# A decoder block on Trainium2: x_proj's B computed by columns, the skip term added through a diagonal matrix, and more scan steps with a row-wise dt·u·B

## The reference: a Mamba pair, an attention, eight experts

```python
u, z = split(x @ in_w.T)                    # 512 channels each
u = silu(causal_dwconv(u, cw, cb))          # 4 taps
dt, Bm, C = split(u @ xp_w.T)               # 16, 64 and 64 columns
dt = softplus(dt @ dtw.T + dtb)             # 512 channels
A = -exp(A_log)                             # 512 x 64
def step(h, (u_t, dt_t, B_t, C_t)):
    h = h * exp(dt_t[:, None] * A) + (dt_t * u_t)[:, None] * B_t[None, :]
    return h, h @ C_t
y = scan(step) + u * D_skip
y = y * silu(z)
out = y @ out_w.T
```

## Time and profile before

| | before |
|---|---|
| median of 3 runs | 3466.93 us |
| profiled execution, its own time | 3468.26 us |
| its span | 3466.5 us |
| mean granted TensorE clock | 0.907 of full speed |
| busy share: VectorE, ScalarE, GpSimd, TensorE | 90%, 81%, 78%, 77% |
| busy VectorE, of which scans, products | 3132.8 us, 2313.6, 710.5 |
| first scan begins, last scan ends | 45.35 us, 3248.9 us |

### The profile page before, as it was taken

How to read it: one execution, slowest core, us unless ns; L and a number is a source line. 1 busy time by engine, 2 the same in 40 slices (tenths; PEclk the granted TensorE clock), 3 DMA queues, 4 the chain that set the end, 5 groups by cost and what they waited for, 6 DMA issues and landing times.

```text
span 3466.5 us, 50869 instructions
## 1 busy us (share of the span) xinstructions
PE 2655.7 (77%) x17556; PEld 2274.8 (66%) x17556; DVE 3132.8 (90%) x2269; ACT 2795.2 (81%) x6418; POOL 2707.2 (78%) x1335
## 2 busy tenths in 40 slices
PE   5767676787777788788787777878878778888876
PEld 3666565666656667677676666767767666777766
DVE  4999999999999999999999999999999999999610
ACT  6979899887989798887888868888797968887422
POOL 5889888887989788787878878787887978877501
PEclk7889998988899899899899988999999879899988
DMA  2242111111111133222242122413323123343486
GB/s 97 86 138 65 46 47 49 52 47 52 47 47 48 48 113 100 81 84 95 73 143 77 68 92 77 140 62 98 122 81 119 50 73 114 99 141 125 136 267 191
DMA packets 148758, 319.64 MB, mean 92 GB/s; under 512 B 25466, under 2 KB 41859, under 8 KB 147988
## 3 DMA queue, kind: packets, MB, share of 16 engines
q1 hardware_dynamic: 144546, 305.60, 26.8%
q0 software_dynamic: 3072, 8.39, 0.7%
q10 hardware_dynamic: 882, 2.38, 0.2%
HBM read 286.42 MB, written 29.88 MB: 91 GB/s over the span
## 4 chain that ended last, share of the span: by engine, by line
issue 32%; DVE 24%; POOL 20%; ACT 12%; PE 11%; DMA 1%; SPq 0%; POOLq 0%; DVEq 0%; ACTq 0%
POOL hC L919 17%; DVE h L1159 11%; DVE psX L1149 10%; ACT dA L1127 5%; ACT xs L1102 2%; PE psY L1422 2%; PE psX L1406 2%; PE psG L1374 2%; PE psX L1374 1%; POOL scratch L832 1%; PE psG L1450 1%; PE psX L1450 1%; DVE gT L1174 1%; POOL gT L842 0%; POOL dtu L855 0%
## 5 line engine op out<-in xcount | busy, mean ns | idle before, releaser
L919 POOL TENSOR_TENSOR hC<-h,cb 128x1024 f32<-128x1024 f32 x1024 | 2405.9, 2366 | 535.0 <-DVE h L1159 526.8
L1159 DVE TENSOR_TENSOR_SCAN h<-dA,psX 128x1024 f32<-128x1024 f32 (+1 forms) x1113 | 2313.6, 2107 | 70.9 <-PE psX L1406 41.9
L1127 ACT ACTIVATE dA<-dt,negA 128x255 f32<-128x255 f32 x4096 | 1717.5, 501 | 124.4 <-DVE h L1159 120.4
L1422 PE MATMUL psY<-ident,hC 128*128 128x128 f32 x8192 | 1186.4, 293 | 61.4 <-DVE gT L1174 41.4
L1422 PEld LDWEIGHTS psY<-ident,hC 128*128 128x128 f32 x8192 | 1041.3, 153 | 96.2 <-DVE gT L1174 44.9
L1406 PE MATMUL psX<-ident,xs 128*128 128x128 f32 x3488 | 537.5, 305 | 300.2 <-ACT xs L1102 150.8
L1149 DVE TENSOR_TENSOR psX<-dtu,psX 128x1024 f32<-128x1024 f32 x588 | 710.5, 1208 | 60.2 <-POOL dtu L855 37.1
L1406 PEld LDWEIGHTS psX<-ident,xs 128*128 128x128 f32 x3488 | 440.3, 156 | 399.7 <-ACT xs L1102 227.4
L1102 ACT ACTIVATE xs<-dtuT,bT 128x512 f32<-128x512 f32 x872 | 579.8, 717 | 9.9 <-PE psX L1406 9.3
L1397 PE MATMUL psX<-bparts,sel 96*128 96x256 bf16 x588 | 172.8, 294 | 238.5 <-DVE h L1159 230.3
L1397 PEld LDWEIGHTS psX<-bparts,sel 96*128 96x128 bf16 x588 | 59.7, 102 | 349.9 <-DVE h L1159 322.0
(11 more groups left out here) (217 smaller groups left out, 1880.1 us busy)
## 6 DMA issues: line engine op xcount, KB each, us to landing
cb<-c_dram SPq DMA_DIRECT2D x256, 512.0 KB
w_up<-in_w_exp SPq DMA_DIRECT2D x198, 256.0 KB
w_down<-in_w_exp SPq DMA_DIRECT2D x198, 256.0 KB
dA<-in_w_exp SPq DMA_DIRECT2D x42, 256.0 KB, 4.2
h<-in_w_exp SPq DMA_DIRECT2D x42, 256.0 KB, 4.4
x_slots<-got SPq DMA_DIRECT2D x16, 512.0 KB, 5.4
xg<-x_slots SPq DMA_DIRECT2D x60, 128.0 KB
y_slots<-yg SPq DMA_DIRECT2D x60, 128.0 KB
```

What stands on the lines that cost most here:

```text
L919: eng.tensor_tensor(hC[i % NHC][:, :, :], h[i % NH][:, :, :], cw.to_broadcast([P, KI, L]), ALU.mult).then_inc(times_c, 1)
L1127: made = eng.activation(dA[j % NA][:, c, 1:L], dt[n % 2][:, c, 1:L], ACT.Exp, scale=negA[:, JOBS[n][0], c, s:s + 1])
L1159: made = eng.tensor_tensor_scan(h[i % NH][:, part, :].rearrange("p c t -> p (c t)"), dA[i % NA][:, part, :].rearrange("p c t -> p (c t)"), ...
L1422: made = eng.matmul(psY[:, tc, c * P:(c + 1) * P], hC[i % NHC][:, c, tc * P:(tc + 1) * P], ident[:, :], start=s == 0 and c == 0, stop=Fals ...
```

## The change

Four edits. B is now computed with positions on the partitions (64 columns, two chunks of positions), and one copy by ScalarE makes `bT` of it; the three bf16 parts, their two GpSimd subtractions, five ScalarE copies, `b_turn` and `sel` are gone. In a plain step `spread_b` takes its row from `bT`: a transpose whose input is the column B_s repeated 128 times, once for each half of the positions. The skip term is added by real f32 products of u with a diagonal matrix of D (`diag`, made once at the start by ScalarE), in the middle of a job, and u is no longer scaled; `gate` waits for the last sum instead. The shares rise to 18 of 30 and 14 of 30: 511 turned steps (221 in the first six jobs, 290 after), and in the first six jobs 70 of them come right behind another turned step. w_x is loaded in three DMAs, which take from the unchanged array only the columns that are used.

```diff
-SHARE = [15] * 6 + [12] * (NJ - 6)
+SHARE = [18] * 6 + [14] * (NJ - 6)
...
-            task("b", n, 0, "PE", 2 * MM, ("silu", n, 0), opens="G"),
-            task("b+", n, 0, "PE", 2 * MM, ("b", n, 0)),
-            task("b", n, 1, "PE", 2 * MM, ("b+", n, 0)),
-            task("b+", n, 1, "PE", 2 * MM, ("b", n, 1)),
-            task("b_hi", n, 0, "ACT", 2 * EVICT, ("b+", n, 1), *((("b_rest", n - 1, 0),) if n else ()), frees=("b", n, 0)),
-            task("b_rest", n, 0, "POOL", 1200, ("b_hi", n, 0)),
-            task("b_mid", n, 0, "ACT", EVICT, ("b_rest", n, 0)),
-            task("b_rest2", n, 0, "POOL", 1200, ("b_mid", n, 0)),
-            task("b_lo", n, 0, "ACT", 2 * EVICT, ("b_rest2", n, 0))]
+            task("b", n, 0, "PE", 8 * TURN, ("silu", n, 0), opens="G"),
+            task("b+", n, 0, "PE", 8 * TURN, ("b", n, 0)),
+            task("bT_copy", n, 0, "ACT", 330, ("b+", n, 0), frees=("b", n, 0))]
...
-    out.append(task("skip", n, 0, "ACT", 4 * HALF_EVICT, ("dtu", n, 1), ("c_copy", n, 0), ("b_hi", n, 0)))
...
-                    at["PE"] = sum_end[j] = max(at["PE"], c_end[j]) + SUM * (2 if j % S == S - 1 else 1)
+                    at["PE"] = sum_end[j] = max(at["PE"], c_end[j]) + SUM * (3 if j % S == S // 2 else 1)
...
-            eng.dma_start(w_x[:, :, :, :], io["w_x"]).then_inc(mamba_in, 16)
+
+            for to, at, many in ((0, 0, HALF), (HALF, 3 * HALF, HALF), (S, 6 * HALF, S + R)):
+                eng.dma_start(w_x[:, :, :, to:to + many], io["w_x"][:, :, :, at:at + many]).then_inc(mamba_in, 16)
...
-                        k, at = turn["b_turn", n, 0]
+                        k, at = turn["b", n, 0]
                         on.wait_ge(full[k], at + 1)
+                        on.wait_ge(x_in, S * (n - 1))
                         eng.activation(bT[n % 2][:, :, :], bank[k][:, 0:KL * S].rearrange("p (a s) -> p a s", a=KL),
                                        ACT.Copy).then_inc(free[k], 1)
...
-                    elif name == "skip":
-                        on.wait_ge(dtu_done, 2 * (n + 1))
-                        for c in range(KI):
-                            made = eng.activation(u[n % 2][:, c, :], u[n % 2][:, c, :], ACT.Identity,
-                                                  scale=dskip[:, JOBS[n][0], c:c + 1])
-                        made.then_inc(skipped, 1)
...
+            on.wait_ge(set_up, SETUP + 1)
+            for l in range(LAYERS):
+                for c in range(KI):
+                    made = eng.activation(diag[:, l, c, :], ident[:, :], ACT.Copy, scale=dskip[:, l, c:c + 1])
+            made.then_inc(diag_made, 1)
...
-                on.wait_ge(b_lo_done, n + 1)
+                evicted(("b", n, 0))
                 on.wait_ge(scanned, i - 1)
-                eng.matmul(psX[i % 2][:, KI - 1, :], sel[:, s % HALF:s % HALF + 1].to_broadcast([3 * HALF, P]), bparts[n % 2][:, s // HALF, :],
-                           start=True, stop=True).then_inc(x_in, 1)
+                for tc in range(KL):
+                    made = eng.transpose(psX[i % 2][:, KI - 1, tc * P:(tc + 1) * P], bT[n % 2][:, tc, s:s + 1].to_broadcast([P, P]), ident[:, :])
+                made.then_inc(x_in, 1)
...
             def add_skip(n):
-                on.wait_ge(skipped, n + 1)
+                on.wait_ge(diag_made, 1)
+                on.wait_ge(silued, n + 1)
                 for tc in range(KL):
                     for c in range(KI):
-                        made = eng.matmul(psY[:, tc, c * P:(c + 1) * P], u[n % 2][:, c, tc * P:(tc + 1) * P], ident[:, :],
-                                          start=False, stop=True, is_transpose=True, skip_group_check=True)
-                    made.then_inc(y_done, 1)
+                        eng.matmul(psY[:, tc, c * P:(c + 1) * P], u[n % 2][:, c, tc * P:(tc + 1) * P], diag[:, JOBS[n][0], c, :],
+                                   start=False, stop=False, skip_group_check=True)
...
-                        made = product(dst[0:3 * HALF, part * L:(part + 1) * L],
-                                       [(w_x[:, l, c, part * 3 * HALF:(part + 1) * 3 * HALF], u[n % 2][:, c, :])
-                                        for c in (2 * i, 2 * i + 1)], not second, second)
-                        if part == i == 1:
+                        made = product(dst[:, i * S:(i + 1) * S], [(u[n % 2][:, c, i * P:(i + 1) * P], w_x[:, l, c, 0:S]) for c in range(KI)])
+                        if second:
                             made.then_inc(full[k], 1)
...
                 if j >= 0:
+                    if j % S == S // 2:
+                        add_skip(j // S)
                     sum_states(j)
-                    if j % S == S - 1:
-                        add_skip(j // S)
```

78 lines of the change are left out of this document (14 added, 64 removed).

## The result

The changed kernel takes **3389.56 us** (median of 4 runs, 3385.51 to 3395.4) beside 3467.88 us (median of 4, 3465.08 to 3469.7) for the kernel before: ratio 0.9774, 95% interval 0.9761 to 0.9788. The profiled execution took 3395.4 us, its span is 3393.7 us, and the mean granted clock rose from 0.907 to 0.928. It is the slowest of the four, 5.8 us above the median, so a few us in a stretch of one trace can be the execution and not the kernel.

A forecast was written before the change was run, and what follows sets the result against it. VectorE was taken to bound the loop (97.0% busy in the first six jobs, 96.6% after). From 3468.3 us, loop -70, head -4 and tail 0 give 3394, less 1.3 to the median: 3393 us, range 3362 to 3436.

The forecast's parts named there:

- The mechanism: In the loop VectorE sets the pace; 75 products fewer remove 90.6 us of its work, 70 us of it gained.
- rival on the slower side: Two, early jobs: TensorE's clock stays low (3554 us, chance 0.03); turned pairs stall 2.13 us each (3542 us, 0.04).
- The early jobs: First six jobs: VectorE's work falls to 1078.3 us, idle share 4.5%, giving 1129 us, a gain of 26 us.
- The pair: Two turned steps in a row, 70 times early: nearly free, 0.1 us each, bounds 0 and 2.13 us.
- take over as the bound: Rival in the early jobs: ScalarE, 1031 against VectorE's 1078 us, bounds them; 26 us lost, 3419 us, chance 0.15.
- The late jobs: Last ten jobs: VectorE's work falls to 1931.3 us, idle share 3.7%, giving 2005 us, a gain of 44 us.
- beside scans, so this shortens nothing by itself: Loop: removing B's chain on ScalarE (76.4 us) and GpSimd (about 37 us) gains nothing directly, only room for scalings.
- The skip, valued at nothing: Skip term moved from a job's last step into step 32: 0 us, bounds -18 and +35 us.
- The tail: After the last scan: three expert tiles more, partly hidden; 0 us against 217, between -8 and +24 us.
- full dovetailing: Tail: expert tiles fill TensorE's gap after the last scan, 209 us against 217, -8 us.
- The head: Uncovered chain before the first scan: shorter B product, one small copy, one subtraction gone; -4 us, bounds -1 and -6.
- three terms valued at nothing: B's chain in the loop, the skip's move into step 32 and the tail, each taken as 0 us.

The follow-up runs named there:

- b_alone: Kernel before with only B by columns and the transposed spread; old shares, old skip term and scaled u kept: 3444.37 us, 0.9923 of the kernel before.
- skip_end_old_plan: Changed kernel with only the issue of the skip products moved to a job's last step, planner's allowance left in place: 3379.47 us, 0.9735 of the kernel before.
- late_share: Changed kernel with shares 15 of 30 in the first six jobs and 14 in the others, only late shares raised: 3409.55 us, 0.9835 of the kernel before.

## Why the prediction came out as it did

The forecast was 3393 us (range 3362 to 3436), the result 3389.56 us.

**The mechanism was right.** VectorE set the pace, and what left it came off the loop. Products 513 and 619.2 us (forecast 513, about 620), scans 2306.7 (2314), ScalarE 2805.8 (2820), the scan's psX waits 56.7 us (50 to 80), the skip 31.8 us (35). The loop ended near 3156 us, 19 us before the 3175 of the forecast, and for that the tail was 20 us longer. Neither rival on the slower side came: the clock rose, and the pairs cost 0.37 us, below the point of about 1 us where they would decide.

**The early jobs, right, with the reason shifted.** -22.7 us for -26. The idle share is 59.8/1132.3 = 5.3%, I took 4.5%. The pair was the mis-sized term, 0.1 us against 0.37. The working found a pair free even with turns of 1.97 us, because it gave TensorE nothing else to do. But 12 of the 21 us at second steps came at step 4, where the turns are queued behind the sum that waits for the gate and then run at the lower clock (1.91 us at 241.69 in job 1). The 2.2 to 2.6 us at step 28 of four jobs are the wait behind the SiLU that the earlier trace rows had shown once; here the second step of the pair often waits 1.1 us more. ScalarE did not take over as the bound: it is busy 90.1% of the stretch. The 96% of the prediction was a share of VectorE's work, and by that measure it is 95% (1019.9/1072.2).

**The late jobs, mis-sized: -69.7 us for -44.** I let the idle share rise from 3.4 to 3.7%; it fell to 2.4%. The path through the runs: B alone -24.0 us (2048.5 to 2024.5), skip edit +13.6 (2038.1), late share -54.8 (1983.3), early share's effect on the layout -4.5 (1978.8). The step that failed is "beside scans, so this shortens nothing by itself" on B's chain. Its waits in the earlier trace rows, spread waits of 22.6 us above all, looked too small to matter one by one. In b_alone, with five ScalarE copies and two GpSimd subtractions per job gone, the late spread waits fell from 14.6 to 4.5 us, and all of VectorE's late waits from 47.9 to 27.2 us. So 21 of the 24 us are waits that went, nearly all from the half of the job in which the chain ran. How much of that is the chain itself, and how much another layout of the tasks or the shorter product of B on TensorE, stays open: every run that changes the list of tasks changes the layout as well. The late share, for its part, gave 55 us where its products are 48, while four tiles left the loop.

**The skip, valued at nothing; its place was a loss of some 10 us.** I bounded it from -18 to +35 us and looked for the delay in step 32, where nothing happened. The cost arose where the work was taken *from*. The earlier trace rows had the slow turn (1.97 us) and the earlier trace rows the clock; neither was connected with what TensorE does just before.

The Trainium skill (TensorE: Matmul & The Clock Gate, Part 4: PE-mode transpose) says that transposes don't count for the clock as products do. The trace agrees only in part: with more transposes and fewer plain products in the spread the mean clock rose from 0.907 to 0.928, and a stretch of 95 us of the change in which TensorE does nothing but transposes was granted 0.89:

```profile
151.00:246.00 95.00, 65.81 (x470) 58.09 (x469) 92.09 (x51) 78.36 (x174) 79.51 (x34) 0.89 0.41 137
```

But 16 rows of real products ahead of the gate did lift the boundaries from 0.68 to 0.91. Whether it was their kind or only that TensorE worked longer and then waited less (2.23 instead of 2.97 us), no run here separates: before and b_alone, with eight transposes in that place (1.14 us instead of 2.0) and waits of 2.76 and 2.75 us, stand between at 0.76 and 0.80. Nor is the wait all: of the four waits of 2.8 us in skip_end_old_plan two were followed by 1.00 and two by 0.76.

**The tail, mis-sized: +19.9 us for 0,** inside its bounds of -8 to +24. I had counted on full dovetailing and on the end of the gap behind the last scan. The work did move in front (56.7 of 62 us), but the gap came from the order of two tasks in the tail's plan and from one buffer, not from a lack of work. It cost what the surplus of the late jobs gave: two errors of 26 and 20 us with opposite signs made the total right, and that was luck.

**The head: -0.4 us for -4.** TensorE's products of before, then of after, each with the busy time of the stretch from 34 us on (clock third from the right), then those of late_share, which has the code of after there:

```profile
34.33 2.37 PE L1374 MATMUL psG<-cdt,shared 17*128 17x256 f32 x8
...
34.00:37.00 3.00, 2.58 (x10) 1.33 (x8) 0.00 (x0) 2.56 (x5) 1.15 (x1) 1.00 0.75 249
```

```profile
30.50 3.51 PE L1327 MATMUL psG<-w_x,u 128*128 128x64 f32 x16
33.94 3.78 PE L1327 MATMUL psG<-cdt,shared 17*128 17x256 f32 x8
...
34.00:38.00 4.00, 4.00 (x11) 2.79 (x11) 0.00 (x0) 2.20 (x5) 0.00 (x0) 0.50 0.84 241
```

```profile
30.78 1.89 PE L1327 MATMUL psG<-w_x,u 128*128 128x64 f32 x16
32.61 1.99 PE L1327 MATMUL psG<-cdt,shared 17*128 17x256 f32 x8
```

B's product took 3.5 us where I took 3.1, which saves a microsecond of the 7.07; the dt product behind it took 3.78 instead of 2.37 us and ate that; and the chain's first product came 0.9 us later (28.21 against 27.33 in the earlier trace rows). The first two are the clock again: the dt product ran at a granted clock of 0.50 in this execution and at 1.00 before. In late_share the two products took 1.89 and 1.99 us, and its head 42.6 us, 2.7 less than before. Of the twelve traces with the new B, five have the dt product at 3.78 us (heads 44.9 to 47.7 us, mean 46.6) and seven at 1.99 us (42.6 to 44.9 us, mean 44.2). So the work that I took off the head did go; what I had not reckoned with is that TensorE may do this chain at either clock. Which of the two an execution gets I can't say, as the same code had both.

## What to carry to other kernels

Before taking work off a busy engine's place in a chain, ask what it did for the engine beside its result: here two microseconds of products ahead of a wait shortened it and went with the upper clock behind it; without them the clock was mostly down just when the next job's fills were due. A sum can be right through errors that cancel, so compare stretch by stretch, and judge parts by runs of each part alone: three terms valued at nothing were worth -24 (B's chain), +10 (the skip's place) and +20 us (the tail). Where a planner lays out the work, any removed task changes the whole layout; separate "same layout, other place" from "new layout" before giving the cause a name.
